# A per-batch conditional MLP on one core: shorter warm-up, first weights rounded in halves, EPS on GpSimd for the first tiles

## The chip, the cores and the metric

One core of one Trainium2 chip runs the whole program. The metric is the device time of one execution in microseconds, the median of three runs.

## What is computed

The input x is 16 batches of 512 rows by 512 features, in float32. Each batch carries a condition 0, 1 or 2, and goes through one of three MLPs; then x is added and each row is normalized.

```python
out_nr  = gelu(x @ w1_nr  + b1_nr)  @ w2_nr  + b2_nr      # condition 0
out_tsr = gelu(x @ w1_tsr + b1_tsr) @ w2_tsr + b2_tsr     # condition 1
h       = gelu(x @ w1_sr  + b1_sr)                        # condition 2, 1024 hidden
h       = gelu(h @ w2_sr  + b2_sr)
out_sr  = h @ w3_sr + b3_sr
y = x + (the one of the three that the batch's condition names)
out = (y - mean(y)) * rsqrt(var(y) + EPS) * gamma + beta
```

The GELU is the exact one. The conditions of this input are 0 2 0 0 0 0 0 1 2 2 1 2 0 2 2 1.

## The kernel before

**Number format.** Every float32 operand is split into two TensorE operands: `hi`, the value rounded to the engine's fp32r format, and `lo`, the remainder. A product is then three matmuls: hi by hi, hi by lo, lo by hi. So every tile of x, of the weights and of the hidden layer is first rounded (ScalarE, VectorE or GpSimd) and then has its remainder taken (VectorE or GpSimd).

**Tiles.** A batch has four 128-row tiles `t`, the features four chunks of 128, and a matmul moves 512 columns. A batch of kind NR (condition 0) or TSR (1) needs 96 real matmuls, one of kind SR (2) 240. The kinds above make 2400.

**Engines.** All five engines run hand-written streams with semaphores. SyncE issues the loads of x (`stage`, in two halves per batch), the weights (`w_raw`, 36 chunks in 18 pairs, resident after the first batches), the rows of x for the residual (`y`) and the stores. ScalarE rounds x (L420, L444), does the GELUs (L415 into `g_hi`, L416 in place) and multiplies by the inverse deviation (L437). VectorE takes remainders (L467, L472, L560), adds the residual (L482), and makes the statistics (L487, L491), the variance plus EPS (L499) and the centring times gamma (L494). GpSimd rounds and splits the later weights (L590, L595, L606), adds the output bias to x (L616), raises the variance to -0.5 (L620, in the last batch L624) and adds beta (L628).

**The start.** TensorE first runs matmuls on a constant, into bank 7, whose results nobody reads: `N_WARM` of 512 columns (L373), then `N_WARM_SHORT` of 128 (L375). Meanwhile SyncE issues, one after the other, x chunk 0, weight chunk 0, x chunk 1, weight chunk 1 (256 KB each, L194 and L195), the second half of x (L190, 512 KB) and the next weight pair (L176, 512 KB). ScalarE rounds x chunks 0 to 3 and then weight chunks 2 and 3 as they land (L444); VectorE rounds weight chunks 0 and 1 (L570) and takes the remainders (L560). TensorE's first batch goes by chunk `c`: for c = 0 and 1 twelve matmuls each (L283), four hi by hi, four with the x remainder, four with the weight remainder. Chunks 2 and 3 follow. It waits on `s_first` (x rounded), `s_first_w` (weight rounded) and `s_nr` or `s_x01` (remainders).

**The end of a batch.** On VectorE tiles are handled in pairs, t = 0 with 1 and t = 2 with 3: two residual adds, two statistics, two moments, then one `variance` instruction for both, then two centrings. GpSimd's `deviations` waits for that variance; ScalarE waits for the centring (`s_v`) and the deviation (`s_rstd`), scales four tiles, and only then comes to the GELUs of the next batch. In batch 0 GpSimd splits weights of kind SR between its bias adds and its deviations. The last batch has its own, tile-by-tile body.

Of the kernel before, what the change touches and what calls it, by code (L numbers as in the profile page):

```python
# [5 lines left out]
P = 128  # L6
NBATCH = 16
T = 512
H = 512
HC = H // P  # L10
TT = T // P
EPS = 1e-5
# [27 lines left out]

N_WARM, N_WARM_SHORT = 9, 14


def conditional_mlp(nc, x, x_t, cond, weights, bias_cols, rows, out):
# [3 lines left out]
    with ctx:  # L48
# [3 lines left out]
        def sem(name):  # L52
            return ctx.enter_context(nc.semaphore(name))
# [35 lines left out]
        s_x_piece = [sem(f"s_x_piece{c}") for c in range(2)]  # L89
        s_w_piece = [sem(f"s_w_piece{c}") for c in range(2)]  # L90
        s_loaded = {(g, n): sem(f"s_loaded_{g}_{n}") for g, (_, count) in PAIRS.items()
# [14 lines left out]
        s_xb, s_ev, s_bn, s_mv = sem("s_xb"), sem("s_ev"), sem("s_bn"), sem("s_mv")  # L106
        s_var = sem("s_var")
        s_own = sem("s_own")
# [60 lines left out]
        def _(eng):  # L169
# [22 lines left out]
            for c in range(2):  # L192
                n = slice(c * T, c * T + T)
                eng.dma_start(stage[:, 0, c, :], x_halves[0][:, n]).then_inc(s_x_piece[c], 16)  # L194
                eng.dma_start(w_raw[:, c, :], weights[0][:, n]).then_inc(s_w_piece[c], 16)  # L195
            load_x(x_halves[1], 1)
# [45 lines left out]
        def _(eng):  # L242
# [42 lines left out]
            def step(kind, read_next):  # L285
                if kind == NR:
                    take(eng, s_x01, 1)
                    for c in range(2):
                        eng.wait_ge(s_first, c + 1)
                        eng.wait_ge(s_first_w, c + 1)  # L290
                        for which in range(3):
                            if which == 1:
                                if c == 0:
                                    eng.wait_ge(s_nr, 1)
                                else:
                                    take(eng, s_x01, 1)
                                    x_taken(0)
                            if which == 2:
                                eng.wait_ge(s_nr, 2 + c)
                            for j in range(HC):  # L300
                                part(j, c, which)
                        if c == 0:
                            read_next()
# [68 lines left out]
            for _ in range(N_WARM):  # L372
                eng.matmul(bank[7][:, :], ones[:, 0:P], ones, start=True, stop=True)  # L373
            for _ in range(N_WARM_SHORT):
# [89 lines left out]
        def _(eng):  # L464
# [50 lines left out]
            def body(kind, read_next):  # L515
                read_next()
                hidden(kind)
                split_x(0, s_x01, 2)
                split_x(1, s_x23, 2)
                eng.wait_ge(s_rows, 16)  # L520
                for t in range(0, TT, 2):
                    residual(kind, t)
                    residual(kind, t + 1)
                    stats(kind, t)
                    stats(kind, t + 1)
                    moments(kind, t)
                    moments(kind, t + 1)
                    variance(t, 2)
                    centre(kind, t)
                    centre(kind, t + 1)  # L530
# [37 lines left out]
            for c in range(2):  # L568
                eng.wait_ge(s_w_piece[c], 16)
                eng.tensor_copy(w_hi[:, c, :], w_raw[:, c, :]).then_inc(s_first_w, 1)  # L570
                x_low(c, c + 1, (s_nr, s_x01)[c])
                eng.wait_ge(s_first_w, c + 1)
                w_low(c, 0)
# [12 lines left out]
        def _(eng):  # L586
# [31 lines left out]
            def deviations(t, n):  # L618
                take(eng, s_var, n)
                eng.tensor_tensor(rstd[:, t:t + n], var_eps[:, t:t + n], power[:, t:t + n], ALU.pow).then_inc(s_rstd, n)  # L620
# [151 lines left out]
```

## Time and profile before

| what | value |
|---|---|
| runs | 558.78, 559.61, 560.52 us; median 559.61 |
| profiled execution | 559.41 us, span 557.7 us, mean granted clock 0.995 |
| TensorE matmul | 549.6 us busy, 99%, 2423 instructions |
| weight load | 453.4 us, 81% |
| VectorE / ScalarE / GpSimd | 273.9 / 213.5 / 248.3 us busy |
| HBM | 44.31 MB read, 16.78 MB written, 110 GB/s |

The span goes from the first to the last instruction of the profiled execution; its own time has 1.7 us more around that. Busy time of TensorE counts overlapping instructions once, and the ends of matmuls are modelled, so the distance between starts tells its rate, not the length of one matmul.

### The profile page before, as it was taken

To read this page: it belongs to the slowest core of one execution; us is meant where nothing else is said; L and a number is where in the kernel's file an instruction comes from. 1 tells how busy PE (TensorE), PEld (TensorE's weight loads), DVE (VectorE), ACT (ScalarE), POOL (GpSimd) and SP (SyncE) were. 2 spreads that over 40 slices of the span, in tenths; PEclk is the share of its full clock that TensorE was granted. 3 is DMA by queue.
4 is the path that set the end of the run, shared out by engine and by line. 5 is a ranking of instruction groups with operands and counts; after the bars stand their busy time and mean duration, and the time that the engine had idled before them with its cause. 6 is when DMAs were issued, how large, how long until landed. Compare 5 with 4: busy or idle time off the path is not lost. (4 is left out here: it accounts for less than half of the span.)

```text
span 557.7 us, 8222 instructions
## 1 busy us (share of the span) xinstructions
PE 549.6 (99%) x2423; PEld 453.4 (81%) x2424; DVE 273.9 (49%) x448; ACT 213.5 (38%) x328; POOL 248.3 (45%) x196
## 2 busy tenths in 40 slices
PE   9999999999999999999999999999999999999994
PEld 6888888888888888888888888888888888888883
DVE  5660176775856956114710569112765105601657
ACT  5451336145244354214421452424255124513351
POOL 0979898765674575300430046600174300430056
PEclk9999999999999999999999999999999999999998
DMA  8876405245344444200320044400244100410032
GB/s 313 339 237 190 152 7 196 100 151 188 109 155 145 156 150 141 84 0 0 138 87 0 1 158 142 150 0 0 75 150 159 66 0 29 154 43 0 0 135 91
DMA packets 26370, 61.28 MB, mean 110 GB/s; under 512 B 3058, under 2 KB 3314, under 8 KB 26226
## 3 DMA queue, kind: packets, MB, share of 16 engines
q1 hardware_dynamic: 26208, 60.97, 31.9%
q8 instruction: 6, 0.10, 0.1%
q10 hardware_dynamic: 146, 0.13, 0.1%
q14 instruction: 10, 0.08, 0.1%
HBM read 44.31 MB, written 16.78 MB: 110 GB/s over the span
## 5 line engine op out<-in xcount | busy, mean ns | idle before, releaser
L467 DVE TENSOR_TENSOR g_lo<-bank,g_hi 128x512 fp32r<-128x512 f32 x112 | 77.5, 692 | 251.0 <-DVEq L117 250.9
L415 ACT ACTIVATE g_hi<-bank,bcol 128x512 fp32r<-128x512 f32 x112 | 77.9, 695 | 165.9 <-ACTq L117 164.7
L620 POOL TENSOR_TENSOR rstd<-var_eps,power 128x2 f32<-128x2 f32 x30 | 21.0, 699 | 239.7 <-POOLq L117 239.7
L616 POOL TENSOR_TENSOR y<-y,row 128x512 f32<-128x512 f32 x64 | 95.7, 1514 | 49.1 <-POOLq L117 48.9
L437 ACT ACTIVATE y<-y,rstd 128x512 f32<-128x512 f32 x63 | 42.3, 717 | 166.3 <-ACTq L117 166.3
L244 PE MATMUL bank<-w_hi,g_hi 128*128 128x512 f32 x256 | 99.6, 389 | 0.0
L245 PE MATMUL bank<-w_lo,g_hi 128*128 128x512 f32 x256 | 99.6, 389 | 0.0
L246 PE MATMUL bank<-w_hi,g_lo 128*128 128x512 f32 x256 | 99.6, 389 | 0.0
L244 PE MATMUL bank<-x_hi,w_hi 128*128 128x512 f32 x240 | 93.4, 389 | 0.0
L245 PE MATMUL bank<-x_lo,w_hi 128*128 128x512 f32 x240 | 93.4, 389 | 0.0
L246 PE MATMUL bank<-x_hi,w_lo 128*128 128x512 f32 x240 | 93.4, 389 | 0.0
L628 POOL TENSOR_TENSOR y<-y,row 128x512 f32<-128x512 f32 x63 | 79.5, 1296 | 0.0
L244 PE MATMUL bank<-g_hi,w_hi 128*128 128x512 f32 x192 | 74.7, 389 | 0.0
L245 PE MATMUL bank<-g_lo,w_hi 128*128 128x512 f32 x192 | 74.7, 389 | 0.0
L246 PE MATMUL bank<-g_hi,w_lo 128*128 128x512 f32 x192 | 74.7, 389 | 0.0
L416 ACT ACTIVATE bank<-bank,bcol 128x512 f32<-128x512 f32 x112 | 74.3, 664 | 0.0
L244 PEld LDWEIGHTS bank<-w_hi,g_hi 128*128 128x128 f32 x256 | 48.1, 188 | 10.0
L245 PEld LDWEIGHTS bank<-w_lo,g_hi 128*128 128x128 f32 x256 | 48.1, 188 | 10.0
L246 PEld LDWEIGHTS bank<-w_hi,g_lo 128*128 128x128 f32 x256 | 48.1, 188 | 9.9
L472 DVE TENSOR_TENSOR x_lo<-stage,x_hi 128x1024 fp32r<-128x1024 f32 x30 | 51.6, 1757 | 4.3 <-DVEq L117 4.3
L245 PEld LDWEIGHTS bank<-x_lo,w_hi 128*128 128x128 f32 x240 | 45.1, 188 | 9.3
L246 PEld LDWEIGHTS bank<-x_hi,w_lo 128*128 128x128 f32 x240 | 45.1, 188 | 9.3
(42 smaller groups left out, 580.2 us busy)
## 6 DMA issues: line engine op xcount, KB each, us to landing
y<-x SPq DMA_DIRECT2D x64, 256.0 KB, 3.6
out<-y SPq DMA_DIRECT2D x63, 256.0 KB, 2.5
stage<-x_t SPq DMA_DIRECT2D x31, 512.0 KB, 3.3
w_raw<-weights SPq DMA_DIRECT2D x17, 512.0 KB, 5.1
row<-rows SPq DMA_DIRECT2D x1, 1280.0 KB, 11.0
stage<-x_t SPq DMA_DIRECT2D x2, 256.0 KB, 3.2
w_raw<-weights SPq DMA_DIRECT2D x2, 256.0 KB, 4.0
out<-y SPq DMA_DIRECT2D x1, 128.0 KB, 1.9
```

The source lines that it names most:

```text
L244: eng.matmul(dst, a_hi, b_hi, start=first, stop=False)
L245: eng.matmul(dst, a_hi, b_lo, start=False, stop=False)
L246: return eng.matmul(dst, a_lo, b_hi, start=False, stop=final)
L415: eng.activation(g_hi[:, slot, :], psum, ACT.Gelu, bias=b)
L416: eng.activation(psum, psum, ACT.Gelu, bias=b).then_inc(s_g, 1)
L437: eng.activation(y[:, t, :], y[:, t, :], ACT.Copy, scale=rstd[:, t:t + 1]).then_inc(s_n, 1)
L467: eng.tensor_tensor(g_lo[:, slot, :], psum, g_hi32[:, slot, :], ALU.subtract).then_inc(s_gs, 1)
L472: eng.tensor_tensor(x_lo[:, c, :], stage[:, f, :, :], x_hi32[:, c, :], ALU.subtract).then_inc(done, n)
L616: eng.tensor_tensor(y[:, t, :], y[:, t, :], row[:, kind, :], ALU.add).then_inc(s_xb, 1)
L620: eng.tensor_tensor(rstd[:, t:t + n], var_eps[:, t:t + n], power[:, t:t + n], ALU.pow).then_inc(s_rstd, n)
L628: eng.tensor_tensor(y[:, t, :], y[:, t, :], row[:, R_BETA, :], ALU.add).then_inc(s_fin, 1)
```

## The change

Five things are changed together. Line numbers behind `@@` are those of before.

- The warm-up is sixteen matmuls of 288 columns and seven of 128, where it was nine of 512 and fourteen of 128.
- Weight chunk 1 is loaded by two DMAs of 256 columns each, with a semaphore each.
- Weight chunks 0 and 1 are rounded by two casts of 256 columns each. TensorE waits for a half before the first two and before the last two of the four hi by hi matmuls, where it waited once for the chunk.
- For t = 0 (tiles 0 and 1) EPS is added by GpSimd just before the power instruction; VectorE only hands on, by a semaphore, that the moments are there. For t = 2 and in the last batch VectorE still does it.
- Nothing else moves; the semaphores `s_moments` and `s_eps` are new.

```diff
-N_WARM, N_WARM_SHORT = 9, 14
+N_WARM, N_WARM_SHORT, WARM = 16, 7, 288
@@ sync
                 eng.dma_start(stage[:, 0, c, :], x_halves[0][:, n]).then_inc(s_x_piece[c], 16)
-                eng.dma_start(w_raw[:, c, :], weights[0][:, n]).then_inc(s_w_piece[c], 16)
+                for h in ((slice(0, T),) if c == 0 else (slice(0, T // 2), slice(T // 2, T))):
+                    eng.dma_start(w_raw[:, c, h], weights[0][:, c * T + h.start:c * T + h.stop]).then_inc(s_w_piece[c, h.start], 16)
@@ tensor, first kind
                         eng.wait_ge(s_first, c + 1)
-                        eng.wait_ge(s_first_w, c + 1)
...
                             for j in range(HC):
+                                if which == 0 and j % 2 == 0:
+                                    eng.wait_ge(s_first_w, 2 * c + j // 2 + 1)
                                 part(j, c, which)
@@ tensor, warm-up
             for _ in range(N_WARM):
-                eng.matmul(bank[7][:, :], ones[:, 0:P], ones, start=True, stop=True)
+                eng.matmul(bank[7][:, 0:WARM], ones[:, 0:P], ones[:, 0:WARM], start=True, stop=True)
@@ vector, body
-                    variance(t, 2)
+                    if t == 0:
+                        take(eng, s_mv, 2)
+                        eng.sem_inc(s_moments, 2)
+                    else:
+                        variance(t, 2)
@@ vector, start
             for c in range(2):
-                eng.wait_ge(s_w_piece[c], 16)
-                eng.tensor_copy(w_hi[:, c, :], w_raw[:, c, :]).then_inc(s_first_w, 1)
+                for half in (slice(0, H // 2), slice(H // 2, H)):
+                    if (c, half.start) in s_w_piece:
+                        eng.wait_ge(s_w_piece[c, half.start], 16)
+                    eng.tensor_copy(w_hi[:, c, half], w_raw[:, c, half]).then_inc(s_first_w, 1)
                 x_low(c, c + 1, (s_nr, s_x01)[c])
-                eng.wait_ge(s_first_w, c + 1)
+                eng.wait_ge(s_first_w, 2 * c + 2)
                 w_low(c, 0)
@@ gpsimd
             def deviations(t, n):
-                take(eng, s_var, n)
+                if t == 0:
+                    take(eng, s_moments, n)
+                    eng.tensor_scalar(var_eps[:, t:t + n], mv[:, t:t + n, 1], EPS, None, ALU.add).then_inc(s_eps, n)
+                    take(eng, s_eps, n)
+                else:
+                    take(eng, s_var, n)
                 eng.tensor_tensor(rstd[:, t:t + n], var_eps[:, t:t + n], power[:, t:t + n], ALU.pow).then_inc(s_rstd, n)
```

VectorE at the start of the program, before:

```order
L570 CAST w_hi<-w_raw 128x512 [waits s_w_piece0]
L560 TENSOR_TENSOR x_lo<-stage,x_hi 128x512 [waits s_first]
L560 TENSOR_TENSOR w_lo<-w_raw,w_hi 128x512 [waits s_first_w]
L570 CAST w_hi<-w_raw 128x512 [waits s_w_piece1]
L560 TENSOR_TENSOR x_lo<-stage,x_hi 128x512 [waits s_first]
```

The same place in the changed kernel, where L579 is the cast and L567 the remainder:

```order
L579 CAST w_hi<-w_raw 128x256 [waits s_w_piece0_0]
L579 CAST w_hi<-w_raw 128x256
L567 TENSOR_TENSOR x_lo<-stage,x_hi 128x512 [waits s_first]
L567 TENSOR_TENSOR w_lo<-w_raw,w_hi 128x512 [waits s_first_w]
L579 CAST w_hi<-w_raw 128x256 [waits s_w_piece1_0]
L579 CAST w_hi<-w_raw 128x256 [waits s_w_piece1_256]
L567 TENSOR_TENSOR x_lo<-stage,x_hi 128x512 [waits s_first]
```

Each cast has become two, and the second chunk's halves wait each for its own DMA.

VectorE in the body of a batch of kind NR, before (tiles 0 and 1, then the start of tiles 2 and 3):

```order
L482 TENSOR_TENSOR bank<-bank,y 128x512 [waits s_xb,s_y]
L487 BN_STATS bn<-bank 128x6 [waits s_ev] x2
L491 BN_AGGR mv<-bn 128x2 [waits s_bn] x2
L499 TENSOR_SCALAR var_eps<-mv 128x2 [waits s_mv]
L494 SCALAR_TENSOR_TENSOR y<-bank,mv,row 128x512 x2
```

The same place in the changed kernel:

```order
L485 TENSOR_TENSOR bank<-bank,y 128x512 [waits s_xb,s_y]
L490 BN_STATS bn<-bank 128x6 [waits s_ev] x2
L494 BN_AGGR mv<-bn 128x2 [waits s_bn] x2
L497 SCALAR_TENSOR_TENSOR y<-bank,mv,row 128x512 [waits s_mv]
L497 SCALAR_TENSOR_TENSOR y<-bank,mv,row 128x512
```

The instruction on `var_eps` is gone there, and the centring follows the moments. GpSimd in batch 0, kind NR, now has it, between its bias adds (L625) and its power instruction (L635):

```order
L625 TENSOR_TENSOR y<-y,row 128x512 [waits s_x_row2]
L625 TENSOR_TENSOR y<-y,row 128x512 [waits s_x_row3]
L631 TENSOR_SCALAR var_eps<-mv 128x2 [waits s_moments]
L635 TENSOR_TENSOR rstd<-var_eps,power 128x2 [waits s_eps]
L599 TENSOR_SCALAR w_hi<-w_raw 128x1024 [waits s_loaded_sr2_0]
L635 TENSOR_TENSOR rstd<-var_eps,power 128x2 [waits s_var]
```

Behind it the order of GpSimd's instructions is what it was.

## Rows read from the trace of the kernel before

**Rows 1.** The page: busy time by engine; granted TensorE clock in 40 slices.

```profile
PE 549.6 (99%) x2423; PEld 453.4 (81%) x2424; DVE 273.9 (49%) x448; ACT 213.5 (38%) x328; POOL 248.3 (45%) x196
...
PEclk9999999999999999999999999999999999999998
```

**Rows 2.** Waits of TensorE: us in total, times, longest us.

```profile
PE bank L373 <- PEq L766: 0.8, 1, 0.8
```

**Rows 3.** TensorE by form, 6.3 us to the end: one of 12 groups.

```profile
L244 PE MATMUL bank<-w_hi,g_hi 128*128 128x512 f32 x256 | 99.6, 389 | 0.0
```

**Rows 4.** Timeline of TensorE: start us, length us, what, count.

```profile
0.82 4.00 PE L373 MATMUL bank<-const-bfloat16-1.0 128*128 128x512 bf16 x9 [0.82 <-PEq L766]
4.61 1.70 PE L375 MATMUL bank<-const-bfloat16-1.0 128*128 128x128 bf16 x14
...
6.07 0.55 PE L283 MATMUL bank<-x_hi,w_hi 128*128 128x512 f32 x1
...
6.46 0.40 PE L283 MATMUL bank<-x_hi,w_hi 128*128 128x512 f32 x1
...
550.01 0.39 PE L246 MATMUL bank<-w_hi,g_lo 128*128 128x512 f32 x1
```

**Rows 5.** Timeline of VectorE and ScalarE, first 10 us, with idle time before.

```profile
4.43 0.43 DVE L570 CAST w_hi<-w_raw 128x512 fp32r<-128x512 f32 x1 [3.53 <-DMA w_raw<-weights]
4.78 0.69 DVE L560 TENSOR_TENSOR x_lo<-stage,x_hi 128x512 fp32r<-128x512 f32 x1
...
7.05 0.43 DVE L570 CAST w_hi<-w_raw 128x512 fp32r<-128x512 f32 x1 [0.99 <-DMA w_raw<-weights]
...
5.54 0.62 ACT L444 CAST x_hi<-stage 128x512 fp32r<-128x512 f32 x1 [1.52 <-DMA stage<-x_t]
8.33 1.14 ACT L444 CAST x_hi<-stage 128x512 fp32r<-128x512 f32 x2 [2.17 <-DMA stage<-x_t]
9.59 1.14 ACT L444 CAST w_hi<-w_raw 128x512 fp32r<-128x512 f32 x2
```

**Rows 6.** Timeline of the weight loads: the first of chunk 1, of chunk 2.

```profile
8.74 0.87 PEld L283 LDWEIGHTS bank<-x_hi,w_hi 128*128 128x128 f32 x4
...
11.46 0.19 PEld L283 LDWEIGHTS bank<-x_hi,w_hi 128*128 128x128 f32 x1
```

**Rows 7.** Timeline of SyncE: the issue of weight chunk 1 and the next.

```profile
2.16 0.43 SPq L195 DMA_DIRECT2D w_raw<-weights  x1
...
2.64 0.43 SPq L190 DMA_DIRECT2D stage<-x_t  x1
```

**Rows 8.** Timeline, 26 to 39 us, engine by engine: end of batch 0.

```profile
27.64 1.14 DVE L499 TENSOR_SCALAR var_eps<-mv 128x2 f32<-128x2 f32 x1
28.70 1.40 DVE L494 SCALAR_TENSOR_TENSOR y<-bank,mv,row 128x512 f32<-128x512 f32 x2
...
26.23 2.53 POOL L616 TENSOR_TENSOR y<-y,row 128x512 f32<-128x512 f32 x2
...
33.33 0.70 POOL L620 TENSOR_TENSOR rstd<-var_eps,power 128x2 f32<-128x2 f32 x1 [2.60 <-POOLq L117]
...
35.88 0.69 ACT L415 ACTIVATE g_hi<-bank,bcol 128x512 fp32r<-128x512 f32 x1 [0.40 <-ACTq L117]
...
37.65 1.47 DVE L467 TENSOR_TENSOR g_lo<-bank,g_hi 128x512 fp32r<-128x512 f32 x2 [3.20 <-DVEq L117]
...
38.66 0.19 PEld L244 LDWEIGHTS bank<-g_hi,w_hi 128*128 128x128 f32 x1
```

**Rows 9.** The centring's line: duration ns min/median/max, first and last start us.

```profile
L494 DVE SCALAR_TENSOR_TENSOR y<-bank,mv,row x64: 734/743/749, 28.7 to 553.1; 128x512 f32<-128x512 f32 x64
```

**Rows 10.** EPS and power by line, as rows 9; ScalarE before tiles 2 and 3.

```profile
L499 DVE TENSOR_SCALAR var_eps<-mv x34: 136/169/1142, 27.6 to 553.1; 128x2 f32<-128x2 f32 x30, 128x1 f32<-128x1 f32 x4
...
L620 POOL TENSOR_TENSOR rstd<-var_eps,power x30: 690/701/723, 29.0 to 533.1; 128x2 f32<-128x2 f32 x30
...
109.40 1.34 ACT L437 ACTIVATE y<-y,rstd 128x512 f32<-128x512 f32 x2 [3.01 <-ACTq L117]
```

More of the change, by code:

```diff
@@ L89, in conditional_mlp @@
         s_x_piece = [sem(f"s_x_piece{c}") for c in range(2)]
-        s_w_piece = [sem(f"s_w_piece{c}") for c in range(2)]
+        s_w_piece = {(c, n): sem(f"s_w_piece{c}_{n}") for c, n in ((0, 0), (1, 0), (1, T // 2))}
         s_loaded = {(g, n): sem(f"s_loaded_{g}_{n}") for g, (_, count) in PAIRS.items()
@@ L106, in conditional_mlp @@
         s_xb, s_ev, s_bn, s_mv = sem("s_xb"), sem("s_ev"), sem("s_bn"), sem("s_mv")
-        s_var = sem("s_var")
+        s_moments, s_eps, s_var = sem("s_moments"), sem("s_eps"), sem("s_var")
         s_own = sem("s_own")
```

## The prediction

> **What bounds the kernel now.** I read the page first: TensorE is busy for 549.6 of 557.7 us, and no other engine passes half [rows 1]. That alone could hide waits, so the view of waits comes next. TensorE's only entry is the 0.8 us before its first instruction [rows 2]. The view of groups from the first real matmul on has 12 groups, 2400 matmuls in all, each with 0.0 us of idle time like the one shown [rows 3]. The timeline gives their rate. The second real matmul starts at 6.46 and the last at 550.01, which is 2398 steps of 226.7 ns [rows 4]. So the kernel is a start, then a solid block of 2400 steps, then 7.7 us of tail behind the last matmul's start. Time can only come from the block starting earlier, from the tail, or be lost where a wait opens in the block.
>
> **The start.** Nine warm-up matmuls of 512 columns run from 0.82 to 4.61, 427 ns each once they run: 512 columns at 1.2 GHz. Fourteen of 128 columns run from 4.61 to 6.07, some 105 ns each, the same level. The first real matmul needs 0.39 us to the next one, and those after it 0.23 us [rows 4]. So the clock rises to the 2.4 GHz level while the first real matmul is in the array. (The granted-clock row prints 9 from its first slice on, so it cannot show this rise [rows 1].) The data was there long before: VectorE finished the rounding of the first weight chunk at 4.86 [rows 5]. What holds the first real matmul until 6.07 is the warm-up itself.
>
> **The change, part by part.**
>
> *Seven short warm-ups fewer.* Sixteen of 288 columns are 4608 columns, exactly nine of 512, so 3.84 us at the same rate. A small matmul carries no visible extra: 128 columns take 105 ns where a quarter of 427 is 107 [rows 4]. Price of the new size: 0. The short ones fall from 14 to 7, and 7 x 107 ns = 0.75 us. The first real matmul moves from 6.07 to about 5.32. What this is worth depends on when the clock rises. If it rises at the same moment as now, the 0.75 us won is filled with real matmuls at 427 ns instead of 227, which are 1.75 matmuls, and 1.75 x 227 ns gives 0.40 us. Counted the other way, 0.75 us less half of it lost to the low level gives 0.37 us. I take **0.37 us**. The upper end is 0.75 us, if the rise came forward together with the real work; the lower end is 0, if a wait swallows it. The trace has one rise only and cannot tell the ends apart. I take 0.37 because TensorE is equally busy up to that point in both kernels.
> The Trainium skill, "TensorE: Matmul & The Clock Gate", Part 1, says that the warm-up is a budget of time and not of matmuls, and that the moment of the rise moves from run to run. By that rule the sum is 0.37 and not 0.75; no second run's trace is here to show the moving.
>
> *The first weight chunk is rounded in halves.* VectorE's one cast of 0.43 us becomes two of 256 columns. Each costs at least half and at most the whole of 0.43, so the x remainder behind them starts 0 to 0.43 us later than 4.78 and ends by 5.9 [rows 5]. TensorE wants it after four matmuls, near 6.5. Price 0. The first two matmuls may go on the first half, near 4.7 instead of 4.9, but TensorE is in its warm-ups until 5.32: gain 0. Without that cover, a chunk landing after 5.1 would leave TensorE idle. Two more waits stand in TensorE's stream in each batch of the first kind; the two that are there now cost nothing [rows 2], so 0.
>
> *The second weight chunk lands in two halves.* SyncE issues one DMA more, 0.47 us by the distance of its issues [rows 7], and every load behind is issued that much later. Issue is not the limit, though: the piece issued at 2.16 is used at 7.05. Landings are what count. The second x piece is used at 5.54, the second weight piece at 7.05, then two loads of double size at 8.33 and 9.59 [rows 5]. So a 256 KB piece took 1.51 us there and a 512 KB load 1.27 us. Time does not go by bytes alone, and smaller rows are not cheaper. Extra delay for all that follows: at least 0 (the same bytes; a gain for the last byte is excluded because the same rows come in more pieces), at most another 1.51 us. I take 0.4, nearer the low end, since the later loads move twice the bytes in less time and so have slack to absorb it.
> Who feels it: TensorE's chunk 2 starts its weight load at 11.46 [rows 6]; the rounded chunk is ready 0.6 us after 9.59, at 10.2 [rows 5]. The margin is 1.26 us, and with TensorE 0.37 us ahead it is 0.89. A delay of 0.4 is covered. For chunk 1 the rounding ends at 7.48 against a need at 8.74 [rows 5, 6]: 1.26, or 0.89 after the change, and its first half comes earlier. Price 0.
>
> *EPS moves from VectorE to GpSimd for tiles 0 and 1.* In most batches this is off every path. VectorE drops an instruction of 0.17 us (median); GpSimd gains it, for something between that and the 0.70 us of its power instruction, plus a wait on itself. The deviations come up to 0.8 us later, and ScalarE, which wants them, then idles 3.01 us before tiles 2 and 3 [rows 10]. Price 0.
> Batch 0 is the place where it matters. There the EPS instruction takes 1.14 us, from 27.64, because GpSimd's two adds run from 26.23 to 28.76, and the centring starts only at 28.70 [rows 8]. The centring itself never stretches: all 64 take 734 to 749 ns [rows 9], many beside GpSimd. So it will start at about 27.65, and tiles 2 and 3 follow 1.0 us earlier. That chain runs on: deviations at 33.33, the first GELU of batch 1 at 35.88, its remainder on VectorE from 37.65 to about 38.35 (the first of two in 1.47 us), and TensorE's layer-2 weight load at 38.66 [rows 8]. The margin is 0.3 us, and this chain starts from loads and GpSimd's adds, not from TensorE. A block 0.37 us earlier would eat it whole and wait some 0.07 us. With the EPS split the margin is 0.3 - 0.37 + 1.0 = 0.93 us. So this part earns nothing by itself; it keeps the 0.37.
> The Trainium skill, "SBUF — State Buffer", in its rule on the shared port pair, says that VectorE and GpSimd lock each other out for whole instructions in some forms, and the 1.14 us agrees. By it GpSimd could be blocked in turn by VectorE, which would lengthen its new instruction but not this chain.
>
> *The tail* runs on code that is not changed and follows TensorE's last matmul. Price 0.
>
> **Sum.** -0.37 us. Against the profiled execution (span 557.7, time 559.41) that is 559.04. The median of the three runs is 0.20 above that execution, so the forecast is 559.61 - 0.37 = 559.24, put as **559.2 us**. The three runs spread over 1.74 us, nearly five times the gain. A measurement of this kernel can tell about 0.3%, 1.68 us, from no change; the forecast is therefore "within 0.3%".
>
> **Rivals.**
> - *Nothing is left of it* (0.18): a margin I priced at 0 is thinner in most runs, for instance the layer-2 one, so the block waits 0.3 us or more once. For it: 0.3 us was thin. Against: the stretched EPS instruction is certainly gone. 559.6.
> - *The rise comes forward too* (0.08): the full 0.75 us. Against: nothing in the trace ties the rise to the real work. 558.9.
> - *Slower, by the halves* (0.06): each half takes as long as the whole piece did, 1.51 us more. The rounded chunk 2 is ready at 11.7 against a need at 11.1, TensorE waits 0.6 us, and 0.6 - 0.37 is +0.25: 559.9. It decides from a delay of 0.89 us on. For it: the 1.51 us piece. Against: the double-size loads at 1.27. The Trainium skill, "DMA: Bandwidth & Descriptors", section Bandwidth, tells one to batch transfers; an estimate between its 64 KB and 1 MB rows makes two halves some 0.6 us dearer than one piece, which would still be covered here.
> - *The clock rises a stretch later* (0.05): with 0.75 us less of warm-up TensorE meets a load that has not landed, goes idle, and must work as long again at the low level. The rise took about 5.5 us of steady work; half of another 5.5 is 2.7, less 0.37: 561.9. For it: the cover over the first weight chunk shrinks from 1.2 to 0.5 us.
> - *The clock rises earlier* (0.05), because sixteen matmuls with sixteen weight loads look busier than nine. All 5.5 us at the high level would give 2.7 us, so up to 556.5, and past the 0.3% bound from some 2.6 us of earlier rise on. Nothing in the trace speaks for it.
>
> **How the numbers follow.** Forecast 0.58. Faster by over 0.3% is only the last rival, 0.05; slower by over 0.3% only the one before it, 0.05; all else, 0.90, is within. The range goes from 558.86 (the full gain) less 0.5 us of run spread to 559.86 (the slow halves) plus 0.4: 558.4 to 560.2.
>
> **What would show it.** Right: the first real matmul near 5.3, real matmuls at 0.43 us each until about 6.4, no wait on TensorE's list, the centring of batch 0 at about 27.7 with no EPS instruction before it, and the first GELU of batch 1 about a microsecond earlier. Wrong: a gap at chunk 1 or 2 or before layer 2 of batch 1, ScalarE's cast of weight chunk 2 starting over 0.9 us later than 9.59, or low-level matmuls far beyond 6.5.

## The result, and the profile after

The changed kernel is slower. Its median is 560.84 us (560.42 to 561.15) against 559.61 (558.78 to 560.52) before, twelve runs of each, ratio 1.0022 with a 95% interval of 1.0015 to 1.0030. The forecast was 559.2, and the range ended at 560.2. One statement of the prediction did hold, that the time would stay within 0.3%: 1.23 us are 0.22%. It held for no reason that the prediction gave.

| what | before | after |
|---|---|---|
| profiled execution, span | 559.41, 557.7 us | 560.8, 558.8 us |
| TensorE matmul | 549.6 us, x2423 | 549.4 us, x2423 |
| first real matmul | 6.07 us | 5.32 us |
| last matmul | 550.01 us | 551.15 us |
| from there to the span's end | 7.7 us | 7.7 us |

The page hides it: TensorE is as busy as before [rows 1], with the same row of granted clock.

```profile
PE 549.4 (98%) x2423; PEld 453.5 (81%) x2424; DVE 271.9 (49%) x435; ACT 213.6 (38%) x328; POOL 252.3 (45%) x211
...
PEclk9999999999999999999999999999999999999998
```

The view of waits shows it. Where TensorE had one entry [rows 2], it now has this one more (total, times, longest in us):

```profile
PE bank L246 <- PEq L117: 1.3, 1, 1.3
```

L246 is the first hi by hi matmul of a step's first product, and the place is in the timeline of TensorE (start, length, what, idle time before it in brackets):

```profile
0.82 4.00 PE L376 MATMUL bank<-const-bfloat16-1.0 128*128 128x288 bf16 x16 [0.82 <-PEq L781]
4.61 0.95 PE L378 MATMUL bank<-const-bfloat16-1.0 128*128 128x128 bf16 x7
5.32 1.49 PE L285 MATMUL bank<-x_hi,w_hi 128*128 128x512 f32 x4
...
27.34 0.39 PE L248 MATMUL bank<-w_hi,g_lo 128*128 128x512 f32 x1
29.02 0.47 PE L246 MATMUL bank<-x_hi,w_hi 128*128 128x512 f32 x1 [1.29 <-PEq L117]
29.32 0.39 PE L247 MATMUL bank<-x_lo,w_hi 128*128 128x512 f32 x1
...
551.15 0.39 PE L248 MATMUL bank<-w_hi,g_lo 128*128 128x512 f32 x1
```

The start is what the prediction said [rows 4]. Up to 27.34, the last matmul of batch 0, the block runs 0.43 us ahead; before, the same matmul is this one (timeline of TensorE of the kernel before):

```profile
27.77 0.39 PE L246 MATMUL bank<-w_hi,g_lo 128*128 128x512 f32 x1
28.00 0.39 PE L244 MATMUL bank<-x_hi,w_hi 128*128 128x512 f32 x1
```

Then the step from 27.34 to 29.02 takes 1.68 us instead of 0.23, so 1.45 are lost. The steps behind it lose a little more, 0.30 against 0.23 us in the first. From 0.43 ahead the block falls 1.02 behind (29.02 against 28.00), and 1.14 by the last matmul.

What TensorE waits for there is its own sequencer (the part that reads the instructions and hands them to the array), and no semaphore. At the end of a batch's code the sequencer jumps out of it to the end of the loop, and goes from there by short tests into the code of the next batch's kind. Here is the first of these jumps by its line, cut to 23 to 28 us: duration min, median, max in ns, first and last start. First the kernel before, then the changed one:

```profile
L390 PEldq COMPARE_BRANCH  x1: 449/449/449, 23.9 to 23.9; - x1
```

```profile
L393 PEldq COMPARE_BRANCH  x1: 3620/3620/3620, 23.5 to 23.5; - x1
```

The branch has become 3.17 us longer, and the sequencer, which is 3 to 4 us ahead of the array here, comes too late. Of the sequencer's 60 branches in the changed kernel it is the only one over 0.5 us. The view of DMA shows what goes with it. Queue q8 carries instructions, in packets of 16 KB. From 20 to 22 us the kernel before has one (packets, MB, share of 16 engines; first fence), the changed kernel none (second); its first comes in the window 24 to 26 (third).

```profile
q1 hardware_dynamic: 413, 0.77, 103.7%
q8 instruction: 1, 0.02, 3.3%
```

```profile
q1 hardware_dynamic: 410, 0.78, 105.0%
```

```profile
q1 hardware_dynamic: 135, 0.46, 59.6%
q8 instruction: 1, 0.02, 3.2%
```

By the packets' own records the first starts at 21.34 before and at 24.53 after, and takes 1.05 and 1.03 us. The held branch ends 1.56 us behind its packet's end: 24.53 + 1.03 is 25.56, and 23.50 + 3.62 is 27.12. From there to batch 1's first matmul it is another 1.9 us (29.02 - 27.12; 1.83 to 1.90 in the other kernels with the gap).

These two numbers give an estimate of the slack of before. Its branch ends at 23.94 + 0.45 = 24.39. The array wants batch 1 at 28.00, so the branch could have ended at 26.1, 1.7 us later. The packet ended at 22.39 and would have let the branch through at 23.95, 0.45 us before it ended anyhow. So the packet could come 2.15 us later than it did before the array lost anything, and 1.7 us with the block 0.43 ahead. It came 3.19 later, less 0.02 for its own length: 3.17 - 1.7 is the 1.45 us. (The two numbers come from this kernel, so this only adds up; below, e3 and e11 test it.)

### The profile page after: what moved, and what is told of

It is laid out like the page before. It is cut to its first block and busy times, and to the rows that moved or that the text cites. A ratio compares the mean times of both kernels' runs of the same rounds, so it can differ in the third digit from the quotient of the medians.

```text
span 558.8 us, 8255 instructions
## 1 busy us (share of the span) xinstructions
PE 549.4 (98%) x2423; PEld 453.5 (81%) x2424; DVE 271.9 (49%) x435; ACT 213.6 (38%) x328; POOL 252.3 (45%) x211
## 5 line engine op out<-in xcount | busy, mean ns | idle before, releaser
L625 POOL TENSOR_TENSOR y<-y,row 128x512 f32<-128x512 f32 x64 | 96.3, 1523 | 47.6 <-POOLq L117 47.2
L246 PE MATMUL bank<-w_hi,g_hi 128*128 128x512 f32 x256 | 99.6, 389 | 0.0
L246 PE MATMUL bank<-x_hi,w_hi 128*128 128x512 f32 x240 | 93.5, 389 | 1.3 <-PEq L117 1.3
L631 POOL TENSOR_SCALAR var_eps<-mv 128x2 f32<-128x2 f32 x15 | 3.3, 218 | 185.5 <-POOLq L117 185.4
L246 PE MATMUL bank<-g_hi,w_hi 128*128 128x512 f32 x192 | 74.7, 389 | 0.0
L246 PEld LDWEIGHTS bank<-w_hi,g_hi 128*128 128x128 f32 x256 | 48.0, 188 | 10.1
L246 PEld LDWEIGHTS bank<-x_hi,w_hi 128*128 128x128 f32 x240 | 45.1, 188 | 11.1 <-issue 1.7
```

Of the source, the lines that this page charges most:

```text
L246: eng.matmul(dst, a_hi, b_hi, start=first, stop=False)
L625: eng.tensor_tensor(y[:, t, :], y[:, t, :], row[:, kind, :], ALU.add).then_inc(s_xb, 1)
L631: eng.tensor_scalar(var_eps[:, t:t + n], mv[:, t:t + n, 1], EPS, None, ALU.add).then_inc(s_eps, n)
```

## The experiments

All medians are of 5 to 12 executions, and each ratio is to 21 to 35 executions of the kernel before that ran beside them (medians 559.52 to 559.81). Packet, branch and lost are of one profiled execution each. "Packet" is the start of the first 16 KB instruction packet behind the start of the program, "branch" the duration of the branch at the end of batch 0, "lost" what TensorE's step before batch 1 takes over 0.227 us.

| kernel | median us | ratio to before (interval) | packet us | branch ns | lost us |
|---|---|---|---|---|---|
| before | 559.61 | | 21.34 | 449 | 0 |
| after | 560.84 | 1.0022 (1.0015, 1.0030) | 24.53 | 3620 | 1.45 |
| e1, whole load | 560.75 | 1.0017 (1.0008, 1.0026) | 24.53 | 3700 | 1.53 |
| e2, before and halves load | 559.82 | 1.0000 (0.9992, 1.0009) | 21.04 | 443 | 0 |
| e3, before and 7 short | 559.69 | 1.0005 (0.9996, 1.0013) | 23.33 | 2383 | 0.16 |
| e4, after with 14 short | 560.95 | 1.0021 (1.0012, 1.0030) | 24.37 | 3440 | 1.27 |
| e5, after with 32 x 144 | 559.54 | 1.0003 (0.9994, 1.0012) | 19.80 | 449 | 0 |
| e6, before and EPS | 559.45 | 0.9990 (0.9981, 0.9999) | 21.43 | 449 | 0 |
| e7, before and warm-up | 559.52 | 0.9998 (0.9989, 1.0007) | 22.06 | 609 | 0 |
| e8, after without EPS | 561.02 | 1.0023 (1.0014, 1.0032) | 24.62 | 3726 | 1.56 |
| e9, after with 16 x 336 | 560.94 | 1.0027 (1.0017, 1.0038) | 25.12 | 3606 | 1.43 |
| e10, after, one cast | 559.46 | 0.9999 (0.9990, 1.0008) | 21.20 | 449 | 0 |
| e11, before and rounding | 560.80 | 1.0025 (1.0014, 1.0036) | 24.60 | 2586 | 0.41 |
| e12, code earlier | 561.78 | 1.0048 (1.0034, 1.0062) | 19.70 | 350 | 0 |
| e13, after, one wait | 559.30 | 0.9993 (0.9984, 1.0002) | 20.94 | 449 | 0 |
| e14, e10 and a late count | 561.01 | 1.0023 (1.0014, 1.0032) | 24.60 | 3634 | 1.46 |
| e15, e18 with 36 x 128 | 560.34 | 1.0011 (1.0002, 1.0020) | 24.14 | 3549 | 1.32 |
| e16, wait in chunk 0 | 560.79 | 1.0017 (1.0008, 1.0026) | 24.45 | 3574 | 1.40 |
| e17, wait in chunk 1 | 559.35 | 0.9993 (0.9984, 1.0002) | 20.62 | 449 | 0 |
| e18, before, EPS, warm-up | 559.10 | 0.9991 (0.9981, 1.0000) | 20.69 | 449 | 0 |

### First: which part of the change brings it

**e1**, the changed kernel with weight chunk 1 loaded whole.

```diff
-                for h in ((slice(0, T),) if c == 0 else (slice(0, T // 2), slice(T // 2, T))):
+                for h in (slice(0, T),):
```

> The changed kernel with the second weight chunk loaded by one DMA again; warm-up, rounding in halves and EPS split stay. In the changed kernel TensorE's jump at the end of batch 0 took 3.62 us, and the one 16 KB instruction packet that it waited for started at 24.53; in the kernel before it started at 21.34. Theory A (the later loads delay the instruction packet): the jump falls back under 0.5 us, the block has no gap, and the time is 559.2, that is 1.6 under the changed kernel. Theory B (the shorter warm-up or the moved EPS brings it about): the jump still takes over 3 us and the time stays near 560.8. The loads behind land some 0.8 us earlier in either case.

The loss stays. ScalarE's casts of x chunks 2 and 3, which come next in the queue, start at 8.94 here (timeline of ScalarE):

```profile
8.94 1.14 ACT L447 CAST x_hi<-stage 128x512 fp32r<-128x512 f32 x2 [1.66 <-DMA stage<-x_t]
```

and in the changed kernel, with the halves, at 9.10:

```profile
9.10 1.14 ACT L447 CAST x_hi<-stage 128x512 fp32r<-128x512 f32 x2 [1.68 <-DMA stage<-x_t]
```

That is 0.16 us of delay in this pair of profiles. Most of the lateness against 8.33 [rows 5] is not theirs: e1 has it too. One pair says little here. Over all profiles, one for each kernel, the cast starts between 8.33 and 9.12 in the eight kernels with the whole load (median 8.83), and between 8.63 and 9.59 in the twelve with halves (median 9.09), so the halves cost some 0.3 us.

**e2**, the kernel before with the halves load alone.

> The kernel before with only the load of the second weight chunk in two halves; VectorE waits for both and rounds as before. Theory A: the loads behind land 0.8 us later, the instruction packet slips behind 24 us, the jump takes over 3 us and the kernel needs 1 to 1.5 us more than before, near 560.8. Theory B: no gap, since the rest is as before; the time is 559.6, the same as before.

No gap and no change of time. The halves load is cleared.

**e3**, the kernel before with seven short warm-ups for fourteen, and **e4**, the changed kernel with fourteen for seven.

```diff
-N_WARM, N_WARM_SHORT = 9, 14
+N_WARM, N_WARM_SHORT = 9, 7
```

> The kernel before with 7 short warm-ups for 14, nothing else. Theory A: the loads are as before, so the jump stays under 0.5 us and the kernel gains the 0.37 us of the prediction, less what the layer-2 margin of 0.3 us takes: 559.2 to 559.4. Theory B (an earlier TensorE meets the jump before its instructions are there): the jump takes over 3 us and the time is 560.5 or more.

> The changed kernel with 14 short warm-ups again, so TensorE's block starts near 6.07 and all else is as changed. Theory A: the loads are as late as in the changed kernel, the packet starts near 24.5, and since the end of the gap is set by it and not by TensorE, the gap is 0.4 us shorter and the time is 560.8 as in the changed kernel. Theory B (shorter warm-up is the cause): no gap and 559.6.

e4 keeps the loss, so the missing short ones are not its cause. e3 has part of it: its packet comes 2.0 us later than before's, its branch takes 2383 ns, and TensorE loses 0.16 us. It gains nothing on before. The sum of slack comes near this: 1.99 us later, less 1.74 (2.15 less the 0.41 that e3's block is ahead at 27.36), leaves some 0.25.

**e5**, the changed kernel with thirty-two warm-ups of 144 columns.

> The changed kernel with its sixteen warm-ups of 288 columns cut into thirty-two of 144: the same columns, the same time by the rows of before, but sixteen matmuls more, so every later instruction of TensorE stands 32 places further on in its stream (each matmul is a weight load and a matmul). Theory C (the jump at the end of batch 0 waits for a 16 KB piece of code that is asked for when the stream passes a fixed place in itself, and the answer comes late because the queue of data loads is full until 24 us): the place is passed some 3 us earlier, the packet starts earlier than 24.5, the gap of 1.45 us closes wholly or by at least half, and the time is 559.3 to 560.0. Theory D (the EPS split or another moved wait holds TensorE there): the gap and the 560.8 stay.

The columns are the same and sixteen matmuls more stand ahead of the real code. The packet comes at 19.80 and the profile has no gap. But the eleven runs fall in two groups, six from 559.03 to 559.54 and five from 560.32 to 560.91. The first group has the profile without the gap; no execution of the second was profiled, so that the gap is there in these five is read from their times alone. If it is, it is not tied to the program's text alone.

**e6**, **e7**: the kernel before with the EPS split alone, and with the new warm-up alone. **e8**: the changed kernel without the EPS split.

> The kernel before with the EPS split alone: GpSimd adds EPS for tiles 0 and 1. Theory C: code and loads of TensorE are as before, so the time is 559.7 as before, or up to 0.3 less. Theory D: the jump at the end of batch 0 waits over 3 us and the time is 560.7.

> The kernel before with the changed warm-up alone, sixteen of 288 columns and seven of 128. TensorE's stream has the same number of instructions as before and reaches every place 0.4 us earlier while the loads stay. Theory C: the code is asked for 0.4 us earlier against the loads, which gives it another place between them; if an earlier request is served later, as the traces so far suggest, the packet starts at 24.5 and the time is 560.7, and if not 559.3. Theory D: 559.3, no gap.

> The changed kernel without the EPS split: VectorE adds EPS for all tiles as before. Theory C: the jump waits as in the changed kernel, the gap is there and the time is 560.8. Theory D: the gap is gone and the time falls to 559.3 to 559.7, with a short wait of under 0.3 us before layer 2 of batch 1, since the 1.14 us EPS instruction of batch 0 is back.

Neither part alone brings the gap, and the changed kernel has it without EPS. The warm-up alone gained nothing in e7's profile, because weight chunk 0 came late. TensorE stood idle for 0.80 us until it was rounded:

```profile
6.24 0.93 PE L283 MATMUL bank<-x_hi,w_hi 128*128 128x512 f32 x3 [0.80 <-DVE w_hi L570]
```

**e9**, the changed kernel with 336 columns for 288, which holds TensorE back by 0.64 us at its first real matmul (5.97).

> The changed kernel with its sixteen warm-ups 336 columns wide instead of 288: 0.6 us more warm-up, not one instruction more or less. Theory C (the request for the code piece meets the queue of loads at a bad moment because TensorE is ahead): TensorE reaches every place up to 0.6 us later, the request falls behind the end of the second x load as in the kernel before, the jump waits under 1 us, and the kernel gets faster by warming up longer: 559.5 to 559.9. Theory D (some part other than TensorE's timing holds the jump): the gap stays, 560.8 to 561.1.

The packet comes 0.59 us later as well, and the gap stays. So the loss is not a matter of TensorE being 0.4 us earlier against the loads, which was my theory when the halves load had fallen away.

### Second: what in the rounding does it

**e10**, the changed kernel with one cast for each chunk, which gives both counts at once. TensorE's code is the changed kernel's, word for word.

```diff
-                for half in (slice(0, H // 2), slice(H // 2, H)):
-                    if (c, half.start) in s_w_piece:
-                        eng.wait_ge(s_w_piece[c, half.start], 16)
-                    eng.tensor_copy(w_hi[:, c, half], w_raw[:, c, half]).then_inc(s_first_w, 1)
+                for start in (0, H // 2):
+                    if (c, start) in s_w_piece:
+                        eng.wait_ge(s_w_piece[c, start], 16)
+                eng.tensor_copy(w_hi[:, c, :], w_raw[:, c, :]).then_inc(s_first_w, 2)
```

> The changed kernel with each of the first two weight chunks rounded by one cast again (its load in halves, the warm-up and the EPS split stay); TensorE's two waits per chunk are both met by that one cast. Theory C: timing of TensorE and of the loads is as in the changed kernel, so the gap and 560.8 stay. Theory D, with the rounding in halves as the part: no gap, 559.3 to 559.7.

**e11**, the kernel before with the rounding and the waits in halves, and nothing else.

> The kernel before with the rounding of the first two chunks in halves alone, and TensorE's waits on halves. Theory C: TensorE starts at 6.07 as before, so no gap, 559.6. Theory D, with this part: the jump waits over 3 us and the time is 560.8.

Taking the rounding in halves away heals the changed kernel; adding it alone makes the kernel before as slow. In e11's profile the step before batch 1 shows only 0.41 us of this, since weight chunk 0 came late there and the first real matmul started at 6.79 instead of 6.07. The packet at 24.60 sets when batch 1 starts (29.05, against 29.02 in the changed kernel), so a late start hides in the gap. By the sum of slack the packet is 3.23 us late for its end, and 3.23 - 2.15 - 0.64 (so much is the block behind at 28.41) is 0.44. It is this part, then, and since e10's TensorE runs the same instructions, what differs is when they run. **e12** adds 20 semaphore instructions and the warm-up of 36 times 128 columns, to put the code of the branch further ahead.

> The changed kernel with 60 more instructions of TensorE ahead of the place where the code piece is asked for: the sixteen warm-ups are thirty-six of 128 columns (the same 4608 columns, 40 places), and 20 increments and decrements of an unused semaphore stand before the last layer of kind NR, where TensorE's sequencer waits for its data anyway. The computation is unchanged. Theory C: the request falls some 3.5 us earlier, near 17 us, the piece is there before the jump even if it has to wait 4 us for its turn, no run has the gap (in e5, with 32 places, about half the runs had it), and the time is 559.1 with all runs under 559.9. Theory D: the gap stays.

The branch has no wait (350 ns), but my 20 instructions cost 2.06 us themselves: they stood behind a wait, and TensorE made a step of 2.29 us at 18.38. The time of e12 says nothing of the cause. Its packet is early, at 19.70, as in e5, which also has more instructions ahead; but TensorE was held as well, and e15 below contradicts that the place of the code is enough.

Which half of the rounding matters, the two casts or TensorE's wait between the four hi by hi matmuls? **e13** keeps the casts and takes the wait in the middle away.

```diff
+                        eng.wait_ge(s_first_w, 2 * c + 2)
                         for which in range(3):
...
-                                if which == 0 and j % 2 == 0:
-                                    eng.wait_ge(s_first_w, 2 * c + j // 2 + 1)
```

> The changed kernel with one thing taken back: TensorE waits once for both halves of a weight chunk (s_first_w at 2c + 2) before its four hi by hi matmuls, where it waited before the first and before the third. VectorE's two half casts stay. Theory E, the wait in the middle is what brings the gap: in the changed kernel the sequencer spent 1.42 us over these matmuls where it spends 1.22 us with a single cast; with one wait the 16 KB instruction packet starts near 21.3, the jump at the end of batch 0 takes under 0.5 us, there is no gap before batch 1's first matmul, and the median is 559.2 to 559.8. Rival, the two casts on VectorE are enough whoever waits for them: packet after 24, jump over 3 us, a step of about 1.7 us near 29, median 560.6 to 561.0.

**e14** keeps the single cast of e10, and gives the second count late, so that the wait in the middle holds TensorE.

```diff
-                eng.tensor_copy(w_hi[:, c, :], w_raw[:, c, :]).then_inc(s_first_w, 2)
+                eng.tensor_copy(w_hi[:, c, :], w_raw[:, c, :]).then_inc(s_first_w, 1)
+                eng.wait_ge(s_first_w, 2 * c + 1)
+                eng.tensor_copy(late[:, :], w_raw[:, c, 0:P]).then_inc(s_first_w, 1)
```

> The version with each chunk rounded by one cast, changed in one thing: the cast gives the first count, and the second count comes from a small extra copy behind it on VectorE (128 columns of the raw weight into a tile that nobody reads). TensorE's code is that of the changed kernel, and its wait in the middle of the four matmuls can now hold it for some 0.2 us. Theory E, that wait brings the gap: packet after 24, jump over 3 us, step of about 1.7 us near 29, median 560.6 to 561.0. Rival, only the half casts themselves do it: jump 0.45 us, no gap, median 559.3 to 559.8, as with the single cast.

Both came out as the theory of the wait has it. The branch of e13, and then of e14, by line from 23 to 28 us:

```profile
L392 PEldq COMPARE_BRANCH  x1: 449/449/449, 23.6 to 23.6; - x1
```

```profile
L394 PEldq COMPARE_BRANCH  x1: 3634/3634/3634, 23.6 to 23.6; - x1
```

In the view of TensorE's waits e14 has the gap (the line below), and e13 has no such line:

```profile
PE bank L247 <- PEq L118: 1.3, 1, 1.3
```

**e16** and **e17** split it once more: the wait in the middle for chunk 0 only, and for chunk 1 only.

```diff
-                                if which == 0 and j % 2 == 0:
-                                    eng.wait_ge(s_first_w, 2 * c + j // 2 + 1)
+                                if which == 0 and j % 2 == 0 and (c == 0 or j == 0):
+                                    eng.wait_ge(s_first_w, 2 * c + (j // 2 + 1 if c == 0 else 2))
```

> The changed kernel, with the wait in the middle of the four hi by hi matmuls kept for chunk 0 only; for chunk 1 TensorE waits once for both halves. In the changed kernel the sequencer loses 0.2 us in chunk 0's group (1.42 against 1.22 us). If the wait in chunk 0 is what defers the packet: packet after 24, jump over 3 us, step of about 1.7 us near 29, median 560.6 to 561.0. Rival, chunk 1's wait does it: jump below 0.5 us, no gap, median 559.2 to 559.6, as with one wait for each chunk.

> The mirror of the one before: the wait in the middle is kept for chunk 1 only, chunk 0 waits once. If chunk 0's wait is the cause: no gap, jump below 0.5 us, median 559.2 to 559.6. Rival, chunk 1's wait does it, or either does: packet after 24, jump over 3 us, median 560.6 to 561.0.

It is chunk 0's. And it is not the length of the hold: e17's wait did hold the sequencer at chunk 1, for 0.95 us between its records at 7.29 and 8.24, where e13 takes 0.60, and nothing came of that. Timeline of TensorE of e16, and then of e17, at the end of batch 0:

```profile
27.30 0.39 PE L248 MATMUL bank<-w_hi,g_lo 128*128 128x512 f32 x1
28.93 0.47 PE L246 MATMUL bank<-x_hi,w_hi 128*128 128x512 f32 x1 [1.24 <-PEq L117]
```

```profile
27.16 0.39 PE L248 MATMUL bank<-w_hi,g_lo 128*128 128x512 f32 x1
27.38 0.39 PE L246 MATMUL bank<-x_hi,w_hi 128*128 128x512 f32 x1
```

The trace also shows the wait itself, where the timeline of matmuls shows none. The sequencer passes chunk 0's first wait and later comes to the load of the next condition behind that chunk's twelve matmuls. In the changed kernel, by line (start in the last columns):

```profile
L303 PEldq EVENT_SEMAPHORE  x2: 51/51/51, 4.9 to 7.5; - x2
```

```profile
L387 PEldq TENSOR_LOAD <-cond_sb x1: 323/323/323, 6.4 to 6.4; - x1
```

From 4.85 to the instruction before that load at 6.28 it takes 1.43 us. It takes 1.22 in before, e10, e13 and e17, 1.42 to 1.43 in e1, e8, e9, e11 and e16, and 1.48 in e14. The 0.2 us leave the array busy, since TensorE is still in its warm-ups when the second half is rounded, at 5.02; in e14, as in e10, the first real matmul takes 0.31 us to the next. The number is no law, though: e5 has 1.42 and half of its runs without the slow time, and the gap is there in e4 with only 1.25, and in e15 with 1.03.

### Third: what the rest is worth

**e15** and **e18** are the kernel before with the EPS split and a shorter warm-up, whole load and whole rounding; e18 has the changed kernel's warm-up, e15 one of thirty-six and seven matmuls, all of 128 columns.

> The kernel before with the EPS split, and with a warm-up of thirty-six matmuls and seven of 128 columns, all 128 wide: 43 places in TensorE's code where 23 stood, 5504 columns where the changed kernel has the same 5504 and before had 6400. Whole load, whole rounding. If the place of the code in its 16 KB blocks sets when the packet is asked for, the packet starts near 19.8, as with the thirty-two warm-ups of 144 columns, and with 1.5 us to spare: no gap at 29 in any run, no second group of runs near 560.6. Median 559.1 to 559.4 if the shorter warm-up's 0.37 us comes through, 559.5 if the landing of weight chunk 0 holds TensorE as it did in most kernels here. Rival, the place does not help a kernel with whole rounding: median 559.6 or more.

> The two parts of the change that cost nothing and promise something, without the rest: the kernel before with the EPS split and the warm-up of sixteen times 288 and seven times 128 columns; whole load, whole rounding. If the shorter warm-up's 0.37 us and the EPS split's margin are all there is: no gap at 29, jump 0.45 us, median 559.2 to 559.4. Rival, the place of the code or the landing of weight chunk 0 takes it back: 559.5 to 560.3, with a packet after 22 or a first real matmul after 5.6.

**e18 is the fastest of all**, 559.10 us, 1.7 us under the changed kernel and 0.9991 (0.9981 to 1.0000) of the kernel before, which is at the edge of what these runs can tell from no change. e15 surprised me: it has no wait in the middle, and still the packet comes at 24.14 and 1.32 us are lost. Its only difference to e18 is the warm-up's cut, twenty matmuls more. So the wait is one way into the gap and not the only one.

## Why the prediction was wrong

**The step that failed** is the last sentence on the first weight chunk: "Two more waits stand in TensorE's stream in each batch of the first kind; the two that are there now cost nothing [rows 2], so 0." The runs put the whole loss of 1.45 us there, and of the two waits on that of chunk 0: e10, e13 and e17 take its holding away and have no gap, e14 and e16 give it back and lose 1.46 and 1.40 us. I priced the wait by what the array would see, and was right that the array sees nothing at 5 us. I did not ask what the sequencer does behind it. Its branch at 23.94 was in the trace of before, and so was the packet that ended 1.55 us ahead of it. I looked at neither, so the 2.15 us of slack there stood in no list of mine, while I worked out margins at each load. None of my rivals was this one either. Of the two on the slower side one put the loss on the loads (e2: nothing), and the other on a clock that rises late (the changed kernel's matmuls are 0.23 us apart from 6.19 on).

**The casts themselves** cost what was said: each half took 0.29 us, and the x remainder behind them started at 4.93 instead of 4.78, long before TensorE wanted it.

**The shorter warm-up, -0.37 us.** Right in the changed kernel's profile: first real matmul at 5.32 as forecast, and 0.43 us ahead by 27.34. As a gain to be counted on it was too sure. In e7 the late weight chunk 0 ate it, and its median is 559.52. "Without that cover, a chunk landing after 5.1 would leave TensorE idle" was the right worry. The one rival with a late load in it had 0.05 and added the low level for a long stretch; e7 idled and then went on at the high one, 0.31 us for its first step and 0.23 for the later ones. VectorE's first cast starts at 4.43 in before [rows 5]; the chunk that it waits for landed at 5.64 in e7 and 6.33 in e11. In sum e13 measured 559.30 and e17 559.35, near the forecast of 559.24, 0.44 and 0.46 under the kernel before that ran beside them. Both ratios are 0.9993 (0.9984 to 1.0002), which these runs can't tell from no change, and e10, without the gap too, is only 0.06 under.

**The clock.** In the changed kernel the low level, 107 ns for 128 columns, lasts up to the first real matmul. That one takes 0.57 us to the next, the second 0.30, and the later ones 0.23. So the rise is near 6.0, about where it was in before (in the step from 6.07 to 6.46), as the prediction had chosen; its sign "until about 6.4" was a little late. In e18, with the same warm-up, it comes within the sixteen, which end by 4.34 instead of 4.61, and the seven need 0.57 us where they needed 0.95:

```profile
0.82 3.68 PE L373 MATMUL bank<-const-bfloat16-1.0 128*128 128x288 bf16 x16 [0.82 <-PEq L775]
4.34 0.57 PE L375 MATMUL bank<-const-bfloat16-1.0 128*128 128x128 bf16 x7
5.17 1.17 PE L283 MATMUL bank<-x_hi,w_hi 128*128 128x512 f32 x4 [0.26 <-DVE w_hi L574]
```

So in e18 the engine was at the 2.4 GHz level before 4.34, at least 1 us earlier, after the same work. "TensorE: Matmul & The Clock Gate", Part 1, of the Trainium skill says that the moment moves from run to run; these two profiles agree, and the sum from one profile's rise was therefore one draw of several.

**The halves load, 0.4 us of delay, covered.** 0.16 us in e1's pair, some 0.3 over all profiles, and covered (e2). The estimate from the Trainium skill, "DMA: Bandwidth & Descriptors", section Bandwidth, some 0.6 us, was too high by either.

**EPS.** The mechanism is right: in the changed kernel GpSimd's instruction takes 0.22 us in all fifteen batches, and the centring follows the moments with 0.25 us of idle time.

```profile
L631 POOL TENSOR_SCALAR var_eps<-mv x15: 217/217/221, 29.6 to 529.8; 128x2 f32<-128x2 f32 x15
```

```profile
27.90 0.41 DVE L494 BATCH_NORM_AGGREGATE mv<-bn 128x2 f32<-128x6 f32 x2
28.56 1.41 DVE L497 SCALAR_TENSOR_TENSOR y<-bank,mv,row 128x512 f32<-128x512 f32 x2 [0.25 <-DVEq L117]
```

The places were later than forecast (28.56 against 27.7, first GELU of batch 1 at 35.76 against about 34.9) because x's and y's loads landed later (x's second half at 21.20 against 20.40, y's first tile at 21.88 against 21.10); e6, whose loads are those of the kernel before, has them late too, at 20.87 and 21.55. Against e8, which lacks only the split, the first GELU is 0.88 us earlier (35.76 against 36.64), and that is the microsecond of the forecast. In e6 the split earned a ratio of 0.9990 by itself, where I had given it nothing: within 0.3%, but its interval ends below 1. The margin before layer 2 was as thin as I read it: e2 and e3, without the split, make a step of 0.49 and 0.40 us that ends at 38.8 and 38.9, e13 and e18 none.

**The tail**: 7.7 us in both, as forecast.

**What stays open.** Why a sequencer that was held for 0.2 us at 5 us gets its code packet some 3.4 us later (21.20 in e10, 24.60 in e14). In the kernels without the gap the packet starts between 19.7 and 22.1, before y's last tiles have landed; in those with it from 23.3 on, mostly when y's last tile has landed (23.90, then 24.53, in the changed kernel). e5's two groups of times suggest that one program can do either, and e15 shows that another cut of the warm-up can bring it without the wait. That the packet was asked for at another time, and that it was asked for in time and served late, are both left; no record shows the request. The kernel does mark each jump ahead, at the start of the batch's code, by a hint (`branch_hint`), and the hint's record (BRANCH_PREFETCH_HINT) decides nothing: it stands at 3.5 us in the changed kernel, e14 and e16, with the gap, and in e10, e13, e17 and e18, without.

## What to carry to other kernels

A semaphore wait can cost more than what the array idles beside it: count the lead of the sequencer over its engine, and look at the branches and the instruction packets of the queue that carries code. Where a program jumps between large bodies while the load queues are full, find the slack of the code packet first: here a hold of 0.2 us far ahead of it cost 1.45 us behind, while one of 0.35 us elsewhere (e17) cost nothing, so try it by a run and don't reckon it by its length. And of several changes made together, run each alone and look for the subset: the warm-up and the EPS split (e18) gave more than all five.

## What the hardware showed that I had not expected

- The branch of TensorE's sequencer took 350 to 449 ns where the first code packet had ended by 22.5 us, and up to 3726 ns where it came later. That packet of 16 KB took 1.02 to 1.05 us, and a held branch was through about 1.55 us after it (e7 too: packet to 23.10, branch to 24.66).
- A wait of 0.2 us that no matmul of e14 sees moved that packet from 21 to 24.5 us (e10 against e14; likewise e13 against e16). One of 0.35 us at the second chunk (e17) left it at 20.62.
- The landing of the same 256 KB at the start of the program moved by almost 2 us from profile to profile (weight chunk 0: 4.41 in before, 5.64 in e7, 6.33 in e11), with the same loads ahead of it. The rounded chunk comes 0.45 us behind the landing, so a warm-up that ends at 5.3 is within that spread.
- A matmul that follows an idle TensorE takes 0.30 us to the next one instead of 0.23 (the one at 29.02 in the changed kernel, whose mean granted clock is 0.997).
